# Flamingo block on one core: value products of six key tiles in one visit, two visits per batch, eight exponential buffers, context items two steps later

## What is computed

```python
q, k, v = proj(layernorm(x), Wq), proj(ctx, Wk), proj(ctx, Wv)      # 16 heads of 16
scores = clip(q @ k.T / 4, -50, 50); scores = where(attend, scores, -50)
probs = softmax(scores)                                              # over 1444 context rows
delta = rs * ((probs @ v) @ Wo.T + bo); delta = norm(delta) * gamma + beta
x = x + tanh(g_xattn) * delta
h = silu(quant(layernorm(x)) @ quant(w1).T) * (quant(x_norm) @ quant(w2).T)
out = x + tanh(g_ffn) * (quant(h) @ quant(w3).T)
```

## Time and profile before

| | |
|---|---|
| median of 3 runs | 1347.72 us (1346.01 to 1348.87) |
| profiled execution, its span | 1347.5 us (no time lies around it that the median has and the span has not) |
| PE busy, share | 1303.3 us, 97% |
| PE weight loads busy | 1207.4 us, 90% |
| DVE, ACT, POOL busy | 1114.3, 964.8, 443.3 us |
| mean granted clock of TensorE | 0.985 |
| one batch in the middle | 40.0 us |

### The profile page before, as it was taken

The page is one execution under the profiler, slowest core; times in us unless marked ns, Lnnn a source line. Parts: engine busy times, 40 slices in busy tenths (PEclk is TensorE's granted clock), DMA queues, the critical chain, the costliest instruction groups (busy, mean ns, idle before and its releaser), DMA issues.

```text
span 1347.5 us, 48025 instructions
## 1 busy us (share of the span) xinstructions
PE 1303.3 (97%) x19984; PEld 1207.4 (90%) x19984; DVE 1114.3 (83%) x2248; ACT 964.8 (72%) x1617; POOL 443.3 (33%) x751
## 2 busy tenths in 40 slices
PE   5999999999999999999999999999999999999993
PEld 4988999999999999999999999999999999999982
DVE  5878888888888888888888888888888888888864
ACT  3776777677777777777777777767777777777761
POOL 3323333323334322333332334332333332333310
PEclk9999999999999999999999999999999999999985
DMA  8867677667777767777767767766767776767630
GB/s 227 195 154 169 162 187 169 161 166 171 164 185 174 166 164 168 173 169 178 168 164 174 173 157 187 173 162 164 174 154 191 172 166 165 173 165 177 148 74 9
DMA packets 142511, 222.15 MB, mean 165 GB/s; under 512 B 29194, under 2 KB 135630, under 8 KB 142286
## 3 DMA queue, kind: packets, MB, share of 16 engines
q1 hardware_dynamic: 128632, 198.78, 61.3%
q0 software_dynamic: 12288, 19.69, 6.7%
q10 hardware_dynamic: 1366, 0.53, 0.2%
HBM read 54.00 MB, written 3.28 MB: 43 GB/s over the span
## 4 chain that ended last, share of the span: by engine, by line
PE 89%; SPq 4%; DVE 3%; DMA 2%; issue 1%; ACT 1%; POOL 0%; DVEq 0%; POOLq 0%
PE sc L1239 22%; PE pvb L1259 20%; PE cb L1294 19%; PE cb L1280 18%; SPq L309 4%; PE mb L1351 3%; PE mb L1320 2%; PE mb L1329 2%; DMA k_st<-k_lo 2%; PE mb L1366 2%; PE mb L1358 1%; DMA c_in<-in_ctxT 0%; PE mb L1313 0%; DVE c_hi L754 0%; PE mb L1335 0%
## 5 line engine op out<-in xcount | busy, mean ns | idle before, releaser
L556 ACT ACTIVATE e_sb<-sc 121x800 f32<-121x800 f32 (+1 forms) x768 | 645.6, 847 | 147.9 <-PE sc L1239 135.3
L1239 PE MATMUL sc<-q_st,k_st 96*121 96x200 f32 (+1 forms) x3072 | 472.2, 276 | 7.1 <-issue 3.0
L1239 PEld LDWEIGHTS sc<-q_st,k_st 96*121 96x121 f32 (+1 forms) x3072 | 411.6, 185 | 34.6 <-issue 8.5
L793 DVE TENSOR_SCALAR e_sb<-e_sb,hi_b 121x1600 f32<-121x1600 f32 (+1 forms) x384 | 399.6, 1048 | 0.8 <-ACT e_sb L556 0.8
L1259 PE MATMUL pvb<-e_sb,v_sb 121*32 121x100 f32 x12288 | 287.6, 251 | 0.0
L1259 PEld LDWEIGHTS pvb<-e_sb,v_sb 121*32 121x32 f32 x12288 | 266.3, 110 | 22.2 <-issue 19.0
L1294 PE MATMUL cb<-wv_hi,c_hi 128*121 128x256 f32 (+1 forms) x768 | 222.1, 289 | 1.6 <-DVE k_lo L784 1.3
L784 DVE SCALAR_TENSOR_TENSOR k_lo<-cb,bk_c,k_hi 128x484 fp32r<-128x484 f32 (+1 forms) x192 | 134.5, 700 | 107.5 <-ACT k_hi L568 107.5
L1294 PE MATMUL cb<-wv_hi,c_lo 128*121 128x256 f32 (+1 forms) x768 | 216.1, 281 | 0.0
L1294 PE MATMUL cb<-wv_lo,c_hi 128*121 128x256 f32 (+1 forms) x768 | 216.0, 281 | 0.0
L470 POOL DMA_DIRECT2D q_st<-bd_hi x256 | 164.0, 644 | 123.7 <-DVE bd_lo L839 120.7
(11 more groups left out here) (160 smaller groups left out, 1508.5 us busy)
## 6 DMA issues: line engine op xcount, KB each, us to landing
k_st<-k_hi SPq DMA_DIRECT2D x512, 121.0 KB, 2.9
c_in<-in_ctxT SPq DMA_DIRECT2D x64, 484.0 KB, 4.0
k_st<-k_lo SPq DMA_DIRECT2D x256, 121.0 KB, 2.9
k_st<-k_hi SPq DMA_DIRECT2D x256, 119.0 KB, 3.5
c_in<-in_ctxT SPq DMA_DIRECT2D x32, 476.0 KB, 4.7
k_st<-k_lo SPq DMA_DIRECT2D x128, 119.0 KB, 3.2
q_st<-bd_hi POOLq DMA_DIRECT2D x256, 50.0 KB, 3.3
q_st<-bd_lo POOLq DMA_DIRECT2D x128, 50.0 KB, 3.3
```

The costliest lines, as they stand in the source:

```text
L556: nc.scalar.activation(e_sb[e_slot(b, n)][0:TL[n], k * SW:(k + 1) * SW].rearrange("p (o c) -> p o c", o=2), sc[q % NSC][0:TL[n], :, 0:2 * PW],
L793: V.tensor_scalar(e, e, E_LO, hi_b[b.par][0:TL[n], n:n + 1], ALU.max, ALU.min).then_inc(clip_done, 1)
L1239: last = T_.matmul(sc[q % NSC][0:TL[n], e // 2, (e % 2) * PW:(e % 2 + 1) * PW], k_st[st_slot(b, n // TPC)][:, pr // NQ, pr % NQ, t0:t0 + T ...
```

## The change

- `VISIT` goes from 4 to 6: visits are at steps 1 and 7, each over six tiles. `NE` goes from 6 to 8. (The second pass keeps 4 and 6.)
- `ITEM` goes from 4 to 6: each context item comes two steps later on TensorE, ScalarE and VectorE.
- On TensorE the visit now stands behind the second scores and the second half of the context item of its step; `h_turn` (step 1) and `x2_turn` (step 7) stand behind it. `delta`, `x_turn`, `x_query` move one step later; the four `up` products take a step each, 8 to 11.
- ScalarE and VectorE follow: `h_turned` and `x2_turned` stand behind the second exponential of their step; the vector steps of the output move by one step or more; `hidden_up` of the second half and `h_max` go to step 0 of the next batch.
- The middle operand of the value products is stored in three slots instead of four (values, ones, values). The two new buffers also hold `care` and `w3s`, and the weights are quantised in another order during the first batch.
- SyncE's and GpSimd's queues keep their order.

```diff
-    NE = 6
-    VISIT = 4
+    NE, NE_CARE = 8, 6
+    VISIT, VISIT_CARE = 6, 4
...
-    ITEM = 4
+    ITEM = 6
...
-        v_sb = sb("v_sb", [TT, NT, NPR, 4, HD])
+        v_sb = sb("v_sb", [TT, NT, NPR, 3, HD])
...
@@ ScalarE, batch
                     exps(b, n, 0)
+                    if nxt and n == 5:
+                        x_turned(c)
+                    if nxt and n == 6:
+                        x_query(c)
+                    if prev and n in (8, 10):
+                        ffn_gate(d, n // 10)
+                    if prev and n in (9, 11):
+                        ffn_up(d, n // 11)
+                    exps(b, n, 1)
                     if prev2 and n == 1:
                         h_turned(b.plus(-2))
-                    if nxt and n == 4:
-                        x_turned(c)
-                    if nxt and n == 5:
-                        x_query(c)
                     if prev and n == 7:
                         x2_turned(d)
-                    if prev and n in (9, 10):
-                        ffn_up(d, n - 9)
-                    if prev and n in (8, 9):
-                        ffn_gate(d, n - 8)
-                    exps(b, n, 1)
...
@@ VectorE, batch
-                    if nxt and n % 4 == 1:
+                    w = n - (ITEM + 1) + (0 if n > ITEM else NT)
+                    of_w = (c if nxt else None) if n > ITEM else (b if own else None)
+                    if prev and n == 2:
+                        attention_out(d)
+                    if nxt and n in (2, 7, 10):
                         split_head(c, n // 4)
-                    if own and n in (ITEM - 3, ITEM - 2):
-                        k_rest(b, NCH - 1, n - (ITEM - 3))
-                    if nxt and n > ITEM and (n - ITEM - 1) % 4 < 2:
-                        k_rest(c, (n - ITEM - 1) // 4, (n - ITEM - 1) % 4)
+                    if of_w and w % 4 < 2:
+                        k_rest(of_w, w // 4, w % 4)
...
@@ TensorE, batch
-                    if nxt:
-                        if n == 4:
-                            x_turn(c, d if prev else None)
-                        if n == 5:
-                            x_query(c)
-                    if prev:
-                        if n == 3:
-                            delta(d, prev2)
-                        if n == 7:
-                            if nxt:
-                                pe.wait_ge(act_x, X_A.after(c, "bd11"))
-                            x2_turn(d)
-                        if n == 8:
-                            up(d, 0, 0)
-                        if n in (9, 10):
-                            up(d, n - 9, 1)
-                    attend()
+                    if prev and n == 4:
+                        delta(d, prev2)
+                    if nxt and n == 5:
+                        x_turn(c, d if prev else None)
+                    if nxt and n == 6:
+                        x_query(c)
+                    if prev and n in (8, 9, 10, 11):
+                        up(d, (n - 8) // 2, n % 2)
+                    scores(b, n, 1)
+                    context(1)
+                    if n % visit == 1 and (n > visit or prev):
+                        attend()
                     if prev2 and n == 1:
                         h_turn(b.plus(-2))
-                    if prev and n == 9:
-                        up(d, 1, 0)
-                    scores(b, n, 1)
-                    context(1)
+                    if prev and n == 7:
+                        if nxt:
+                            pe.wait_ge(act_x, X_A.after(c, "bd11"))
+                        x2_turn(d)
```

More of the change, by code:

```diff
@@ L658, in passes @@
                     ctx_item(whole(0, base), w)
-                    if w >= 3 and not base:
-                        for i in range(2 * w - 6, min(2 * w - 4, 6)):
+                    if w >= 2 and not base:
+                        for i in range(2 * w - 4, 2 * w - 2):
                             magnitudes(i)
@@ L1001, in batch @@
                         clip(d, NT - 1)
[L1002 removed]
+                    if nxt and n == 7:
                         q_rest(c)
[L1004 removed]
+                    if nxt and n in (2, 7, 10):
                         split_rest(c, n // 4)
[L1006 to L1009 removed]
+                    if b.base and of_w and w % 4 >= 2:
+                        v_guard(of_w, w // 4, w % 4 - 2)
                     if prev2 and n == 0:
[L1011 removed]
+                        hidden_up(b.plus(-2), 1)
+                        for step in (h_max, h_scale, h_round, h_quant):
                             step(b.plus(-2))
@@ L1173, in passes @@
                 clip(e, NT - 1)
-                for step in (h_scale, h_round, h_quant):
+                hidden_up(e.plus(-1), 1)
+                for step in (h_max, h_scale, h_round, h_quant):
                     step(e.plus(-1))
@@ L1371, in batch @@
                 first = not prev
+                visit = visit_of(b)
                 for n in range(NT):
-                    group = [(b, i) if i >= 0 else (d, i + NT) for i in range(n - LAG - VISIT + 1, n - LAG + 1)]
-                    has_pv = n % VISIT == 1 and (n > VISIT or prev)
                     def context(half):
@@ L1383, in attend @@
                     def attend():
-                        if has_pv:
-                            for pb, pn in group:
-                                pv(pb, pn, 0, first)
-                                pv(pb, pn, 1, first)
+                        for i in range(n - LAG - visit + 1, n - LAG + 1):
+                            pb, pn = (b, i) if i >= 0 else (d, i + NT)
+                            pv(pb, pn, 0, first)
+                            pv(pb, pn, 1, first)
                     scores(b, n, 0)
@@ L1454, in passes @@
                 batch(e, True, False, True, True)
-                for n in range(NT - VISIT, NT):
+                for n in range(NT - visit_of(e), NT):
                     pv(e, n, 0)
```

77 lines of the change are left out of this document (34 added, 43 removed).

## The result

The changed kernel takes 1542.78 us in the median (1537.69 to 1546.28, 4 runs), the kernel before 1346.87 beside it: a ratio of 1.146, 95% interval 1.143 to 1.149. It is 196 us slower. 1565 was predicted, with a range of 1455 to 1625. The profiled execution has a span of 1544.4 us.

A forecast was written before the change was run, and what follows sets the result against it. TensorE, busy throughout a batch, was taken to bound the kernel. To the profiled 1347.5 us came -3 for visits, 129 for the stack wait, 53 for the `k_lo` wait, 39 for the clock: 1565 us, range 1455 to 1625.

The forecast's parts named there:

- The stack of chunk 0: Next batch's key stack starts late behind step 7's visit; TensorE waits 4.3 us at step 12, 129 us in all.
- The low part of chunk 2's keys: `k_lo` ready 7.4 us after W, step 1's visit end; TensorE waits 1.7 us at step 4, 53 us in all.
- Both waits stand: Stack and `k_lo` waits both count, since a visit lies between them and VectorE restarts from step 1's visit end.
- The clock: TensorE's lull at the stack drops it to 1.2 GHz for 3 to 4 us, 30 times: 39 us, bounds 0 and 57.
- The visits: Two visits of 192 matmuls per batch take 8.64 us like three of 128; edges save 9 us at most, -3 us taken.
- Waits without the clock: Rival, chance 0.17: both waits come, but TensorE's lull leaves the clock up; 1526 us.
- no wait: Rival, chance 0.06: key stack's DMAs start while step 7's visit runs, so no wait; 1338 to 1344 us.
- Only one wait, or short ones: Rival, chance 0.13: walk along ScalarE or VectorE is off, or query stack moves away; 1470 or 1417 us.
- The sign that was set: In the changed kernel's waits, TensorE on the key stack's DMA shows some 30 waits of 3 to 5 us.

The follow-up runs named there:

- query_light2: Changed kernel with GpSimd stacking only the first quarter of the queries' rows from batch 2 on, so scores differ from the reference: 1500.4 us.
- k_first: Changed kernel with VectorE's split of the next batch's chunk 0 moved from step 2 to step 3, behind the low part of the keys: 1578.1 us.
- restored2: Changed kernel with context items one step later instead of two, VectorE's splits and low parts reordered, one low part ahead of step 5's first sum: 1400.8 us.
- x2_first: Changed kernel with TensorE's `x2_turn` ahead of the visit of step 7, nothing else: 1540.9 us.
- split_in_visit: Changed kernel with VectorE's split of the next batch's chunk 0 moved from step 2 into step 1, ahead of `attention_read`: 1516.5 us.
- fill_both: Changed kernel with matmuls whose result is overwritten, 18 ahead of the wait at step 12 and 12 ahead of that at step 4: 1509.9 us.
- restored3: restored2 with the low part of the second key item of chunk 0 ahead of `x1_norm` at VectorE's step 6 instead of step 7: 1369.6 us.
- light_split: Changed kernel with `x2_turn` ahead of step 7's visit, a quarter of the queries' rows stacked, and chunk 0's split in step 1's visit: 1405.4 us.
- visit4: Changed kernel with visits of four tiles again, at steps 1, 5 and 9; later items, eight buffers and new order stay: 1570.0 us.

## Why the prediction was right, by its steps

**The stack of chunk 0.** Mechanism, place and start were right: the copy of x2 behind the visit, then the keys' high part, low part and the DMAs, 1.98 us behind the visit where 2.2 was said. PE's wait is 74.3 us, 87.2 by the weight loads, where 129 was forecast (bounds 72 and 159). The term that was mis-sized is the stack's own time, 12.3 us by the overlap; it took 10.8 in the median, so that a wait is 2.4 and not 4.3 us. That is the forecast's lower bound, which stood for no overlap, but there was one: the query stack started 0.9 us ahead of the visit's end and landed 8.4 of 10.8 us into the key stack. What was wrong is its price. The forecast had 2.9 us for a full overlap, from one turn of the kernel before (13.3; over its 31 turns the stack took 12.7 in the median); with all but a quarter of the query stack left out it took 10.0 instead of 10.8 (query_light2), so most of this overlap cost 0.8 us and not 1.9.

**The low part of chunk 2's keys.** 1.77 us in each batch, 52.5 to 58.2 in all; 1.7 and 53 were forecast. The walk along VectorE was right: its sum was W + 7.6, of which 7.4 was used, and by 737.99 and the end of the low part's accumulator at 745.58 it was W + 7.6; TensorE was there at W + 5.7 (743.29 and 0.41 for the scores), as forecast.

**"Both waits stand."** As an account of the changed kernel it was right. What it suggests, that each can be had back alone, is wrong: k_first and restored2 took one away and paid it at the other. VectorE works from the visit of step 1 to the end of its step 7 without a pause but two for GpSimd of 1.06 and 0.77 us; the query stack and the load start from the end of that stretch, and so does the key stack once the copy of x2 does not hold it (x2_first). Before the change VectorE idled 0.5 us ahead of that stretch, now 5.7 (177.9 in 31), and the copy of chunk 0's split and the first low part of chunk 2, which stood ahead of it, stand inside it. Of the two moves of the same split only the one that took it out of the stretch (split_in_visit) shortened the turn.

**The clock.** 39 us were forecast, behind the waits for the stack alone, one fall in each of 30 turns; the 3 to 4 us at the lower level that the sum used had no row behind them. It falls behind both: in the trace it goes to 1.2 GHz 21 times behind a wait for the stack and 12 times behind one for k_lo, for 3.4 us nearly each time. Half a value item and the scores behind it then take 2.09 us (775.72 to 777.81 in TensorE's timeline) instead of 1.14 (747.72 to 748.86). From the mean clocks, TensorE spends (1 - 0.950) x 2 x 1544.4 = 154 us at the lower level, against 40 before; 114 us at a loss of some 0.45 (0.95 of 2.09) are 51 us. fill_both recovered 33 by filling the waits. So 33 to 51, the forecast's size, from fewer falls at each kind of wait and from two kinds instead of one. Behind waits of the same length it fell in some turns and not in others (of the k_lo waits of 1.73 to 1.78 us, behind 10 of 25), and no run shows what decides. The section that was cited (the Trainium skill, "TensorE: Matmul & The Clock Gate", "HAM oscillation — how this bites in real kernels") had a fall once in every turn of a loop; this trace has it in about half of the places, 33 of 62.

**The visits.** Two of 4.28 us in the median against three of 2.90: 0.1 us a batch gained, some 4 us, about as forecast. But the forecast took a visit of 192 at the pace of one of 128 throughout, and 17 of the 64 visits stop once, 0.17 to 1.25 us from one matmul's start to the next's, 9.5 us in all; none of the 96 before does. All 17 stops lie inside a tile's 32 matmuls, where the code waits for nothing, and from one turn to the next their place mostly moves on by 8 or 9 matmuls. restored3 has 22, 15.3 us in all; here is one of them:

```profile
836.68 0.72 PE L1276 MATMUL pvb<-e_sb,v_sb 121*32 121x100 f32 x23 [0.76 <-issue]
837.33 0.26 PE L1352 MATMUL mb<-identb,x2q 100*128 100x100 bf16 x2
```

Ahead of each of these 39 the trace has a packet of 16 KB of the queue that carries instructions (q8 on the page), ended 1.2 to 1.6 us before TensorE went on; only some 6 in 100 matmuls of all visits start in such a place. That TensorE had run out of instructions is argued from this, not shown. So visits of six do cost something of their own, some 10 to 15 us.

**The rivals.** "Waits without the clock" is out by the trace's 33 falls and by fill_both; "no wait" by the waits. "Only one wait, or short ones" was half right: its sum had 72 and 53 us of waits, and 74 and 52 came; what it lacked was the clock. The sign that was set, some 30 waits of 3 to 5 us, was missed too: the median is 2.4 us.

**The nearness of the sum is partly luck.** It was 22 us too high. The stack's term was 55 too high; against it stand the clock, 12 more than forecast, and two terms that the sum did not have: 9.5 us of stops inside visits and 10 behind the waits, of which next.

**What stays open.** Each wait is some 0.16 us longer from start to start than the idle time shown (743.29 to 745.63 is 2.34, less 0.41 of scores is 1.93, not 1.77): 62 x 0.16 = 10 us. Against the kernel before (2.0 and 1.3 us of the two waits) that gives 72 + 51 + 51 + 9.5 + 10 - 4, some 190 of the 197 us. In light_split 56 us are left by the profiled spans: 10 at the two waits, 12 more in waits of TensorE for x2q (16.2 where 4.4 were before), 6 by the clock, 12 in stops inside visits (22 of them), and some 16 not settled. In restored3 26 are left: 15 in such stops, and two turns of 47.8 and 45.7 us among turns of 41, each with a wait of 3 us of TensorE ahead of scores that the view puts down to nothing.

## What to carry to other kernels

When an engine's order is moved against another's, walk the stretch of the second fullest engine between the two points where it is tied to the first, and count what the move puts into it: transfers start from its end, and a wait removed inside it can come back behind it. Batch the fullest engine's work only if the others have something to do meanwhile; here a visit of 4.3 us left VectorE idle ahead of its longest chain. Before pulling a transfer forward, look at what else the DMA engines then carry.

## What the runs showed of the hardware

TensorE's clock fell to 1.2 GHz for 3.4 us behind idle times of 1.73 to 2.28 us, 12 times, and of 1.7 to 3.6 us, 21 times, and stayed at 2.4 GHz behind others of the same length. Thirty matmuls of no use in each batch made the program 33 us faster. A stack of 12 DMAs of 121 KB took 10.0 us (medians of 31 turns) with a quarter of the query stack beside its start, 10.8 with a query stack that began 2.6 us ahead of it, 12.2 with one that began 1.1 us ahead and most of a load of 484 KB, and 12.7 in the kernel before, with one that began 0.7 us behind its start. In visits of 192 matmuls at 22.5 ns each TensorE stopped once, mostly for 0.2 to 1.3 us, in 15 to 26 of 64 in every kernel here that has them; in the 96 visits of 128 of the kernel before it never did, and in those of visit4 4 times.
